# Both key groups of a head unit in one transfer of 64 rows, in a two-layer Flamingo block on one core

## What is computed

```python
x = x + tanh(g_xattn) * attention(layernorm(x), ctx, w_q, w_k, w_v, w_o)   # 16 heads of 8
x = x + tanh(g_ffn)   * experts(layernorm(x), gate_w, gate_up_w, down_w)   # 8 experts, top 2

# attention:
k = (ctx @ w_k.T).reshape(B, 1500, 16, 8)
attn = softmax(einsum('bqhd,bkhd->bhqk', q, k) * 8 ** -0.5)
```

## Time and profile before

| | |
|---|---|
| median of three runs | 287.26 us (287.11 to 287.62) |
| the profiled execution's own time | 288.83 us |
| its span, first to last instruction | 287.1 us |
| PE busy | 275.0 us (96%) |
| DVE, ACT, POOL busy | 214.3, 182.1, 97.9 us |
| transfers of keys | 102 (68 from `k_high`, 34 from `k_low`) |
| DMA engines, share of their time in SP's queue | 42.7% |

### The profile page before, as it was taken

One profiled execution on the slowest core, in us unless ns is written; L12 is line 12 of the kernel. 1 busy time (PEld: TensorE's weight loads), 2 busy tenths in 40 slices (PEclk: granted clock), 3 DMA queues, 4 the chain that ended last, 5 costly groups with the idle time before them and its releaser, 6 DMA issues.

```text
span 287.1 us, 8051 instructions
## 1 busy us (share of the span) xinstructions
PE 275.0 (96%) x2826; PEld 223.7 (78%) x2826; DVE 214.3 (75%) x419; ACT 182.1 (63%) x370; POOL 97.9 (34%) x114
## 2 busy tenths in 40 slices
PE   7988999999999999999999998999979999999994
PEld 2465778878888887887887888887778879999962
DVE  4678597887977979679788797798446788888761
ACT  2636586677776777578667775466716877776500
POOL 3598732152043033233215201023610655554200
PEclk9999799999999999999999999999999999999999
DMA  7397943961990991693396199300000000000001
GB/s 252 105 203 202 216 107 125 228 191 36 246 259 3 239 240 58 169 243 126 110 243 186 40 218 277 121 0 2 2 2 0 1 0 2 0 1 0 0 0 32
DMA packets 9924, 32.19 MB, mean 112 GB/s; under 512 B 2576, under 2 KB 3088, under 8 KB 9904
## 3 DMA queue, kind: packets, MB, share of 16 engines
q1 hardware_dynamic: 9472, 31.60, 42.7%
q10 hardware_dynamic: 432, 0.33, 0.4%
HBM read 13.26 MB, written 0.23 MB: 47 GB/s over the span
## 4 chain that ended last, share of the span: by engine, by line
PE 86%; DVE 7%; DMA 2%; ACT 1%; issue 1%; POOL 1%; SPq 0%; DVEq 0%; ACTq 0%
PE max_ps L969 16%; PE score_ps L949 15%; PE o_ps L983 14%; PE misc_ps L937 8%; PE misc_ps L931 6%; PE score_ps L1194 3%; PE score_ps L1196 3%; PE score_ps L1195 3%; DVE part_max L706 2%; PE o_ps L1280 2%; PE o_ps L1194 2%; PE o_ps L1195 2%; PE o_ps L1196 2%; PE max_ps L992 2%; PE misc_ps L1107 1%; PE max_ps L999 1%
## 5 line engine op out<-in xcount | busy, mean ns | idle before, releaser
L706 DVE TENSOR_REDUCE part_max<-max_ps 112x1 f32<-112x512 f32 (+1 forms) x192 | 117.4, 671 | 33.4 <-PE max_ps L969 31.7
L517 ACT ACTIVATE probs<-score_ps 128x448 f32<-128x448 f32 x192 | 92.3, 545 | 16.6 <-PE score_ps L949 16.4
L969 PE MATMUL max_ps<-kx,qx 96*112 96x512 f32 (+1 forms) x192 | 82.3, 434 | 2.2 <-DVE part_max L706 1.1
L949 PEld LDWEIGHTS score_ps<-qx,kx 104*128 104x128 f32 (+1 forms) x384 | 69.7, 189 | 10.8 <-issue 2.1
L949 PE MATMUL score_ps<-qx,kx 104*128 104x224 f32 (+1 forms) x384 | 74.3, 278 | 0.6 <-DVE qx L725 0.4
L983 PE MATMUL o_ps<-probs,v_sb 128*32 128x112 f32 (+1 forms) x1536 | 44.5, 261 | 0.6 <-ACT probs L517 0.6
L969 PEld LDWEIGHTS max_ps<-kx,qx 96*112 96x112 f32 x192 | 33.9, 177 | 8.8 <-issue 4.9
L983 PEld LDWEIGHTS o_ps<-probs,v_sb 128*32 128x32 f32 (+1 forms) x1536 | 36.4, 110 | 3.1 <-ACT probs L517 0.8
L366 POOL TENSOR_TENSOR k_low<-k_full,k_high 128x512 fp32r<-128x512 f32 (+1 forms) x21 | 26.2, 1251 | 30.7 <-ACT k_full L500 30.4
L401 POOL TENSOR_TENSOR o_norm<-o_sb,inv_den 128x112 f32 (+1 forms) x15 | 6.3, 423 | 75.8 <-DVE inv_den L732 75.8
L512 ACT ACTIVATE v_sb<-misc_ps 128x512 f32<-128x512 f32 x24 | 14.4, 602 | 27.4 <-PE misc_ps L937 27.4
(11 more groups left out here) (177 smaller groups left out, 367.2 us busy)
## 6 DMA issues: line engine op xcount, KB each, us to landing
kx<-k_high SPq DMA_DIRECT2D x60, 187.5 KB, 5.0
kx<-k_low SPq DMA_DIRECT2D x30, 187.5 KB, 4.9
ctx_sb<-in_ctxT SPq DMA_DIRECT2D x7, 750.0 KB, 5.7
gu_sb<-in_guT SPq DMA_DIRECT2D x8, 512.0 KB, 4.9
dn_sb<-in_dnT SPq DMA_DIRECT2D x8, 256.0 KB, 5.1
ctx_sb<-in_ctxT SPq DMA_DIRECT2D x2, 256.0 KB, 4.2
kx<-k_high SPq DMA_DIRECT2D x4, 123.5 KB, 2.3
kx<-k_high SPq DMA_DIRECT2D x4, 64.0 KB, 2.0
```

Source lines behind the costliest of these rows:

```text
L517: nc.scalar.activation(probs[:, (KT * h + t) % 8, :], score_ps[:, t % 3, 0:SC // 2], ACT.Exp, scale=SCALE).then_inc(exp_done, 1)
L706: nc.vector.reduce_max(part_max[:, p, c:c + 1], max_ps[0:PC, bank, 0:size], AX.X).then_inc(max_taken, turns)
L949: last = nc.tensor.matmul(score_ps[0:m, t % 3, GC * g:GC * g + GC], kx[0:KR, 2 * par + h, g, 128 * t:128 * t + m], qx[0:KR, par, 2 * h + g ...
L969: nc.tensor.matmul(max_ps[0:PC, bank, 0:size], qx[0:MR, par, 2 * h + p // 2, PC * (p % 2):PC * (p % 2) + PC], kx[0:MR, slot, p // 2, start ...
```

## The change

The two groups of a unit move together: a transfer takes 64 rows of `k_high` or `k_low` and writes them to 32 rows of a slot, in both groups' places. Row `2 r + g` of a half goes to row `r` of group `g`. So that this is so, the columns of the key weights are laid out ahead of the launch such that the groups' rows alternate within a half. A unit takes three transfers in place of six (51 in place of 102 in all), each of twice the bytes. The semaphores per group are gone: PE waits for `kx_begun` before product 0 and for `kx_loaded[slot]` before product 4 (first unit) or product 0 (all others), and these count the transfers of both groups. The order of instructions is the same on all engines but for the transfers and one wait per unit that is gone.

```diff
-        kx_begun = [sem("kx_begun0"), sem("kx_begun1")]
-        kx_loaded = [[sem(f"kx_loaded{u}{g}") for g in range(2)] for u in range(4)]
+        kx_begun = sem("kx_begun")
+        kx_loaded = [sem(f"kx_loaded{u}") for u in range(4)]
...
-        def move_keys(eng, par, h, g, part, landed):
+        def move_keys(eng, par, h, part, landed):
+
             start, size = part
-            r = 32 * (2 * h + g)
             for row, src in ((0, k_high), (1, k_low), (2, k_high)):
-                eng.dma_start(kx[32 * row:32 * row + 32, 2 * par + h, g, start:start + size].bitcast(f32),
-                              src[r:r + 32, par, start:start + size].bitcast(f32)).then_inc(landed, 16)
+                eng.dma_start(kx[32 * row:32 * row + 32, 2 * par + h, :, start:start + size].bitcast(f32),
+                              src[64 * h:64 * h + 64, par, start:start + size].bitcast(f32)
+                              ).then_inc(landed, 16)
...
             def move_unit(par, h):
-                for g in range(2):
-                    move_keys(sp, par, h, g, (0, TK), kx_loaded[2 * par + h][g])
+                move_keys(sp, par, h, (0, TK), kx_loaded[2 * par + h])
...
             sp.wait_ge(k_low_saved, 1)
-            for g in range(2):
-                move_keys(sp, 0, 0, g, PARTS[0], kx_begun[g])
+            move_keys(sp, 0, 0, PARTS[0], kx_begun)
             sp.wait_ge(k_low_saved, NCH)
-            for g in range(2):
-                move_keys(sp, 0, 0, g, PARTS[1], kx_loaded[0][g])
+            move_keys(sp, 0, 0, PARTS[1], kx_loaded[0])
             move_unit(0, 1)
...
-                if not first and n % 6 == 0:
-                    pe.wait_ge(kx_loaded[slot][n // 6], MOVES * (i + 1))
+                if not first and n == 0:
+                    pe.wait_ge(kx_loaded[slot], MOVES * (i + 1))
...
             for n in range(UM):
-                if n < HP and n % 2 == 0:
-                    pe.wait_ge(kx_begun[n // 2], MOVES)
-                if n >= HP and n % 4 == 0:
-                    pe.wait_ge(kx_loaded[0][n // 8], MOVES)
+                if n == 0:
+                    pe.wait_ge(kx_begun, MOVES)
+                if n == HP:
+                    pe.wait_ge(kx_loaded[0], MOVES)
...
-        "wkT": layout(np.asarray(L0_xattn_w_k).T),
+        "wkT": layout(np.asarray(L0_xattn_w_k).T.reshape(D, 2, 2, 32).transpose(0, 1, 3, 2).reshape(D, D)),
```

More of the change, by code:

```diff
@@ L504, in keys_moved @@
                 for h in range(2):
-                    for g in range(2):
-                        act.wait_ge(kx_loaded[2 * par + h][g], MOVES * (i + 1))
+                    act.wait_ge(kx_loaded[2 * par + h], MOVES * (i + 1))
             def v_copy(b, par, n):
```

## The result

The changed kernel takes 318.83 us (median of 4 runs, 313.86 to 321.22) where the kernel before takes 287.2: a ratio of 1.098, with an interval of 1.093 to 1.103. The change makes the kernel slower by 10%, and the forecast was 289.8 with a range of 288.0 to 290.8. The sign was right and the size was off by a factor of eleven (28.7 us for a forecast of 2.6).

A forecast was written before the change was run, and what follows sets the result against it. PE was taken to bound the kernel, with key transfers mattering only before product 4. Late keys (+1.8 us) and a low clock stretch (+0.8) gave +2.6 on the median 287.26, so 289.8 us, range 288.0 to 290.8.

The forecast's parts named there:

- The bound and the place: PE holds 86% of the chain, DMA 2%; a key transfer matters only before product 4 of the first unit.
- the saved issues and semaphores: 51 issues of about 0.6 us on SP and one PE wait per unit removed; costed at nothing.
- Term 1: Start phase: product 4 waits for twice the bytes at 211 GB/s, starting at 18.26 instead of 16.47: +1.8 us.
- C: Key moves: wide transfers run faster, up to 414 GB/s, giving 286.9 to 287.6 us; chance 0.12.
- D: Before the loop: the 1.15 us idle no longer leads to low clock, giving back up to 1.7 us; chance 0.08.
- The loop costs nothing: Loop refills: last transfer lands at 57.0, first product needing it starts at 59.12, so 2.1 us of cover.
- the third unit's keys: First filling, issued at about 28.1: landing about 35.3, asked for behind 37, so no wait.
- rival E: A second wait, at the second unit's keys or in the loop: +3.5 us and more, 290.8 to 292; chance 0.02.
- Term 2: PE's clock: the longer idle before product 4 brings one more low stretch, +0.8 us (bounds 0 and 1.7).
- Rival A: The forecast itself: late keys at product 4 and a low clock stretch, 288.8 to 290.8 us; chance 0.55.
- the second unit's keys: Start phase: landing at 24.2, asked for at 24.6, some 0.4 us left; up to 0.3 us cost in the range.

The follow-up runs named there:

- joint waits alone: Kernel before with its 102 transfers of 32 rows; only PE's waits changed, to wait for both groups at once: 290.56 us, ratio 1.011.
- wide transfers across row 64: Changed kernel with half 0's groups alternating in rows 32 to 95, moved wide, and half 1 moved by six 32-row transfers: 291.61 us, ratio 1.012.
- rate alone: Kernel before, still six 32-row transfers a unit and a wait per group, but each reads every second row of 64: 288.7 us, ratio 1.0044.

## Why the prediction was wrong

**The bound and the place were right.** The one transfer of keys in the chain of before was where the loss begins, and no gain from the saved issues and semaphores is to be seen: joint waits alone cost 3.2 us, wide transfers across row 64 with them 4.2.

**Term 1 failed in its rate.** "I take 211, since that row is the nearest: the same source tile, the same destination rows, the same 16 engines, and only more rows of the source." The change moves keys at about 130 GB/s. The landing took 6.74 us from the third issue and not 4.14. I had put the slow end at 192 GB/s, the slowest row for 32 rows, which is no bound on an access pattern that the trace doesn't have. At 211 the term itself holds: with joint waits alone product 4 came at 18.41, and with wide transfers across row 64 at 18.13, for a forecast of 18.26. The Trainium skill's rule in "SBUF — State Buffer", the section on the DMA port swizzle, that 64 rows are served as 32 are, agrees with the copies whose shape stays the same (64 to 64 rows 4.44 us, 32 to 32 4.46). It gave 218 GB/s for the change, and there it isn't borne out: 64 rows to 32 x 2 are at 130 from rows 0 to 63. The Trainium skill's rule in "DMA: Bandwidth & Descriptors", the rules for kernel authors, to make one large transfer of many small ones, gives the wrong sign here: the kernel is 10% slower, because of the new pattern of rows and not of the size, since wide transfers of 375 KB across row 64 keep the rate. The rivals C (a better rate) and D (a gain by the clock) were wrong too.

**"The loop costs nothing" failed, and about half of the loss comes from there.** Wide transfers in the loop alone cost 14.1 us. The cover of 2.1 us was read rightly, and it was priced at an unchanged rate only. An estimate: at 130 GB/s in place of some 205 a slot's 1152 kB take 8.9 us and not 5.6, 3.3 us more, 1.2 above the cover. The traces bear it out: from a refill's first issue to its last landing it was 10.0 us before (47.01 to 57.0), and is 13.4 to 14.0 in the last four refills of the chain. The waits found there are 1.24 to 1.57 us for each batch (2.27 for the first, where the context load went on beside it). The runs of rate alone (+1.3), joint wait alone (+3.2) and both (+13.7) show that it takes both. The same holds for the third unit's keys, which I had landing 2 us early and PE waited 4.18 us for. My rival E had the mechanism, at a chance of 0.02 and with a price of 3.5 us; it is a wait per round and not one wait.

**Term 2 was right in kind and small in size.** The clock fell behind product 4 as forecast, in the kernel with joint waits too, where five of six runs have a mean of 0.993 or 0.994. It isn't certain even so: with wide transfers across row 64 the wait was 2.21 us, and two of four runs have a mean of 1.000. In the changed kernel it fell behind five of the seven waits for keys (4.88, 4.18, 2.27, 1.53 and 1.57 us, and not behind 1.40 and 1.24) and behind the 1.79 us for a context load, and the low clock makes 11.9 of the 30.9 us. The base was off the other way: the profiled execution of before had a low stretch that most of its runs don't have, and the 1.6 us between it and the median are about what term 2 gives for such a stretch. Rival A's upper end leaves out the 0.3 us that it names for the second unit's keys: its own terms give 291.1 and not 290.8, which decides nothing here.

**Open.** Whether the 4 us of the loss that neither place shows alone come with both together or are the scatter of the runs. Why a wide transfer on one side of row 64 is slow and one across it is not, and why stepped sources are slow in steps of two and four and not of three.

## What to carry to other kernels

Before wider or fewer transfers are put in, the rate of the new access pattern is to be measured by itself, in an idle stretch of the same kernel; a row of the old pattern doesn't bound it, and a DMA share near 1 says nothing on it. Each cover that a change leans on is to be priced at the slow end of every rate in the sum, since two edits that cost little alone (a joint wait 3.2 us, a rate lower by a quarter 1.3) may need the same cover (13.7 together). In a loop a wait that exceeds its cover comes back in every round, and PE's clock adds to it.

## What the hardware showed

- Copies within the on-chip memory of 192 kB in 32 rows run at some 200 GB/s. Other choices of source rows for the same bytes, by the same engines, take from 4.2 to 6.2 us a set of three; 128 rows to 128 take 3.46.
- A copy of 64 rows to 32 x 2 runs at about 130 GB/s from rows 0 to 63 or 64 to 127, and at 202 to 248 GB/s from rows 32 to 95.
- By the mean clock of each run, an idle of 1.15 us of PE was followed by a fall of the clock in few executions of the same kernel (two of 56), one of about 2.35 us in most (five of six), and one of about 2.2 us in another kernel not in all (two of four have a mean of 1.000).
